# The last graph product with the adjacency tiles as stationary operand: feature rows come out on the partitions, and the bias, the positive part and the layer norm move with it

## What is computed

```python
def _layernorm(x, axis=-1, eps=1e-05):
    m = jnp.mean(x, axis=axis, keepdims=True)
    v = jnp.var(x, axis=axis, keepdims=True)
    return (x - m) / jnp.sqrt(v + eps)
...
x = _layernorm(x + _L0_gnn_ref(x, adj, adj, ...))     # two gated cells, fed by A @ x and by a graph attention
# _L1_gnn_ref(x, adj, adj, ...)
    sim = jnp.tanh(adj * simlar)                      # simlar is adj again
    filt = sim * (adj > 0).astype(sim.dtype)
    ...                                               # the 350 largest of a row: here every row has fewer
    h2 = jnp.tanh(h @ W_proj + b_proj)
    feat = jax.nn.relu(new_adj @ (h2 @ W_gcn) + b_gcn)
x = _layernorm(x + _L1_gnn_ref(x, adj, adj, ...))
```

## Time and profile before

| what | value |
|---|---|
| median of three runs | 1340.59 us |
| the profiled execution, its own time | 1340.1 us |
| its span | 1338.8 us |
| TensorE busy | 1319.6 us, 99% |
| VectorE, ScalarE, GpSimd busy | 1017.7, 961.3, 93.3 us |
| graph products L1363, busy | 167.0 + 27.8 us (448 instructions of 512 columns), 14.1 + 15.8 us (128 of 256) |
| turns of features L1374 | 32 instructions, 5.1 us busy, 4.6 us idle before |
| granted TensorE clock, mean | 0.997 |

### The profile page before, as it was taken

The page is one execution under the profiler, slowest core; times in us unless marked ns, Lnnn a source line. Parts: engine busy times, 40 slices in busy tenths (PEclk is TensorE's granted clock), DMA queues, the critical chain, the costliest instruction groups (busy, mean ns, idle before and its releaser), DMA issues.

```text
span 1338.8 us, 11264 instructions
## 1 busy us (share of the span) xinstructions
PE 1319.6 (99%) x3700; PEld 610.9 (46%) x3700; DVE 1017.7 (76%) x1331; ACT 961.3 (72%) x1087; POOL 93.3 (7%) x188
## 2 busy tenths in 40 slices
PE   8999999999999999999999999999999999999996
PEld 3444444464444444444444444444444454444455
DVE  2533333448798998999989999899968987788883
ACT  4655556238788988889888898898946666565662
POOL 0000001000000100100100100100103441000000
PEclk9999999999999999999999999999999999999998
DMA  9988887353123242332423424223123347888860
GB/s 370 361 288 283 299 290 279 73 206 135 70 95 141 95 160 92 110 141 95 142 94 106 162 79 151 101 94 104 53 94 108 128 146 251 306 292 308 299 219 18
DMA packets 46706, 228.92 MB, mean 171 GB/s; under 512 B 10610, under 2 KB 16434, under 8 KB 21042
## 3 DMA queue, kind: packets, MB, share of 16 engines
q1 hardware_dynamic: 44080, 225.55, 48.0%
q10 hardware_dynamic: 2562, 2.59, 0.6%
HBM read 223.83 MB, written 4.29 MB: 170 GB/s over the span
## 4 chain that ended last, share of the span: by engine, by line
PE 91%; DVE 4%; DMA 2%; POOL 1%; issue 1%; ACT 1%; SPq 0%; DVEq 0%; ACTq 0%; POOLq 0%
PE t_y_ps L1801 48%; PE ns_ps L422 15%; PE t_y_ps L1363 12%; PE t_y_ps L1779 4%; PE rows_ps L1363 3%; PE t_y_ps L1314 2%; DVE mask L1232 2%; PE t_es_ps L1770 2%; DMA pieces<-in_adj_c 2%; PE t_y_ps L1316 1%; PE pos_ps L436 1%; PE rows_ps L1316 1%; PE t_es_ps L1347 0%; DVE mask L1718 0%; PE t_y_ps L1340 0%
## 5 line engine op out<-in xcount | busy, mean ns | idle before, releaser
L1801 PE MATMUL t_y_ps<-mask,x_sb 128*128 128x512 f32 x1536 | 663.1, 592 | 0.3 <-DVE mask L1718 0.3
L1801 PEld LDWEIGHTS t_y_ps<-mask,x_sb 128*128 128x128 f32 x1536 | 290.1, 190 | 364.2 <-issue 343.0
L1718 DVE TENSOR_TENSOR mask<-mask 128x1536 f32<-128x1536 f32 x256 | 451.1, 1763 | 2.0 <-ACT mask L1602 2.0
L1602 ACT ACTIVATE mask<-mask,ones 128x1536 f32<-128x1536 f32 x256 | 400.3, 1564 | 0.0
L1595 ACT ACTIVATE mask<-mask,pieces 128x512 f32<-128x512 f32 x352 | 241.8, 713 | 31.3 <-PE t_y_ps L1801 28.2
L422 PE MATMUL ns_ps<-pieces,x_sb 128*128 128x512 f32 x504 | 226.3, 602 | 6.0 <-DMA pieces<-in_adj_c 5.6
L1704 DVE TENSOR_SCALAR mask<-mask,e_cols 128x512 f32<-128x512 f32 x416 | 189.2, 489 | 56.4 <-PE t_y_ps L1801 45.3
L1363 PE MATMUL t_y_ps<-mask 128*128 128x512 f32 (+1 forms) x448 | 181.2, 562 | 0.1
L422 PEld LDWEIGHTS ns_ps<-pieces,x_sb 128*128 128x128 f32 x504 | 93.8, 192 | 122.1 <-issue 115.6
L288 DVE TENSOR_SCALAR mask<-pieces 128x2048 fp8e4<-128x2048 f32 x64 | 76.9, 1224 | 92.8 <-DMA pieces<-in_adj_c 74.9
L1232 DVE SCALAR_TENSOR_TENSOR mask<-mask 128x2048 f32<-128x2048 f32 x64 | 142.4, 2285 | 0.9 <-DMA mask<-in_adj_c 0.9
(11 more groups left out here) (176 smaller groups left out, 635.3 us busy)
## 6 DMA issues: line engine op xcount, KB each, us to landing
mask<-in_adj_c SPq DMA_DIRECT2D x128, 1024.0 KB, 4.8
pieces<-in_adj_c SPq DMA_DIRECT2D x63, 1024.0 KB, 5.1
mask<-scratch_shifts SPq DMA_DIRECT2D x8, 1536.0 KB, 7.8
x_sb<-in_x_p SPq DMA_DIRECT2D x8, 256.0 KB, 8.9
mask<-in_x_t SPq DMA_DIRECT2D x1, 2048.0 KB, 17.0
pieces<-in_x_t SPq DMA_DIRECT2D x8, 256.0 KB, 2.9
pieces<-scratch_ns_t SPq DMA_DIRECT2D x8, 256.0 KB, 3.7
scratch_ns_t<-ns_sb ACTq DMA_DIRECT2D x7, 256.0 KB, 5.8
```

Of the source, the lines that this page charges most:

```text
L1602: nc.scalar.activation(t, t, ACT.Exp, bias=ones[:, :], scale=-1.0).then_inc(exped, 1)
L1718: nc.vector.tensor_tensor(term(n), term(n), a, ALU.mult).then_inc(terms, 1)
L1801: mm = nc.tensor.matmul(y_ps[c % 2][h][:, :], x_sb[:, k, :], term(n)[:, h, :], start=k == 0, stop=k == NB - 1)
```

## The change

The graph product changes operands. The stationary side is now a 128 x 128 tile of the adjacency block, the moving side g_all[:, k, :], 128 columns; every block takes four products instead of one, and a result tile has its rows on the partitions. Before the first block of a part, one product of contraction length 1 (a row of ones by b_gcn, repeated for each tile) puts the bias in the bank. relu, turn_features and the squarings on ScalarE are gone; add_x1 reads PSUM, takes the positive part and adds x1 in one instruction. Both layer norms are made from bn_stats and bn_aggr per tile (measure), and subtraction and multiplication are one instruction per tile (normalize). The last chunk is cut in three tiles and one, where it was two and two. SyncE loads b_gcn as a row; its waits for the finished parts count tiles.

```diff
-END_PARTS = [... for c in range(NCHUNK - 1)] + [(NCHUNK - 1, q, q + CHUNK // 2) for q in range(0, CHUNK, CHUNK // 2)]
+END_PARTS = [... for c in range(NCHUNK - 1)] + [(NCHUNK - 1, 0, CHUNK - 1), (NCHUNK - 1, CHUNK - 1, CHUNK)]
...
-        def center(i, y, mu, sem_centered):
-            nc.vector.tensor_reduce(mu, y, AX_X, ALU.add)
-            nc.vector.tensor_scalar(mu, mu, 1.0 / H, None, ALU.mult)
-            nc.vector.tensor_tensor(y, y, mu.unsqueeze(2).broadcast_to([P, count, H]), ALU.subtract)
+        def measure(tiles, buf, out, sem_stats, sem_averaged):
+            for t in range(tiles.start, tiles.stop):
+                nc.vector.bn_stats(buf[:, t, :], x1[:, t, :]).then_inc(sem_stats, 1)
+            for t in range(tiles.start, tiles.stop):
+                dve.wait_ge(sem_stats, t + 1)
+                nc.vector.bn_aggr(out[:, t, :], buf[:, t, :]).then_inc(sem_averaged, 1)
+        def normalize(tiles, out, roots, sem_out):
+            for t in range(tiles.start, tiles.stop):
+                nc.vector.tensor_scalar(x1[:, t, :], x1[:, t, :], out[:, t, 0:1], roots[:, t:t + 1], ALU.subtract, ALU.mult)
...
         def add_x1(i):
-            dve.wait_ge(turned2, i + 1)
-            nc.vector.tensor_tensor(x1[:, tiles, :], back_ps[i % 2][...], x1[:, tiles, :], ALU.add)
+            dve.wait_ge(products, NPIECE * (i + 1))
+            nc.vector.scalar_tensor_tensor(x1[:, tiles, :], f_ps[i % len(f_ps)][...], 0.0, x1[:, tiles, :], ALU.max, ALU.add)
...
             if g == 0 and i >= len(f_ps):
-                pe.wait_ge(relu_done, i - len(f_ps) + 1)
+                pe.wait_ge(y2_done, i - len(f_ps) + 1)
+            if g == 0 and tiles.start == 0:
+                pe.wait_ge(bias_step, 9)
+                nc.tensor.matmul(f_ps[i % len(f_ps)][:, q * P:end * P], one_row[:, :],
+                                 b_gcn_row.unsqueeze(1).broadcast_to([1, end - q, H]), start=True, stop=False)
             for j in tiles:
                 k = g * PIECE + j
-                mm = nc.tensor.matmul(f_ps[i % len(f_ps)][:, q * P:end * P], g_all[:, k, :], piece(u)[:, j * CW + q * P:j * CW + end * P],
-                                      start=k == 0, stop=k == NB - 1)
+                for r in range(q, end):
+                    mm = nc.tensor.matmul(f_ps[i % len(f_ps)][:, r * P:(r + 1) * P], piece(u)[:, j * CW + r * P:j * CW + (r + 1) * P],
+                                          g_all[:, k, :], start=False, stop=k == NB - 1 and r == end - 1)
```

More of the change, by code:

```diff
@@ L1025, in make_biases @@
             nc.vector.tensor_copy(gate_bias[k]["hid_n"], b_hid[:, 2:3]).then_inc(bias_step, 1)
+        nc.vector.memset(one_row[:, :], 1.0).then_inc(bias_step, 1)
     def pool_tail(pool):
         for c in range(NCHUNK):
[L1031 to L1034, removed]
+            at, spread, (t, v, out) = POOL_STEPS * c, moments[:, rows(c), 1], (a[:, rows(c)] for a in (newton, var, root))
+            pool.wait_ge(averaged, CHUNK * (c + 1))
+            nc.gpsimd.tensor_scalar(t, spread, 1.0, EPS, ALU.mult, ALU.add).then_inc(rooted, 1)
+            nc.gpsimd.tensor_scalar(v, spread, -0.5, -0.5 * EPS, ALU.mult, ALU.add).then_inc(rooted, 1)
             pool.wait_ge(rooted, at + 2)
@@ L1112, in tanh @@
             nc.scalar.activation(piece(u), piece(u), ACT.Tanh).then_inc(filtered, 1)
[L1114 to L1125, removed]
         act.wait_ge(bias_step, 8)
@@ L1154, in scalar_tail @@
         copy_g(end - 2)
-        square_x(end)
         make_h2(end - 1)
@@ L1215, in make_y @@
             dve.wait_ge(y_done, CHUNK * (c + 1))
-        def center(i, y, mu, sem_centered):
[L1218 to L1223, removed]
+        def measure(tiles, buf, out, sem_stats, sem_averaged):
[6 more added lines that the diff above has]
+            for t in range(tiles.start, tiles.stop):
+                nc.vector.tensor_scalar(x1[:, t, :], x1[:, t, :], out[:, t, 0:1], roots[:, t:t + 1], ALU.subtract, ALU.mult).then_inc(sem_out, 1)
         def finish_x(c):
             dve.wait_ge(rooted, POOL_STEPS * (c + 1))
-            nc.vector.tensor_tensor(x1[:, rows(c), :], x1[:, rows(c), :], root[:, rows(c)].unsqueeze(2).broadcast_to([P, CHUNK, H]),
-                                    ALU.mult).then_inc(x_done, 1)
+            normalize(rows(c), moments, root, x_done)
         def square_a(u):
@@ L1263, in finish_y @@
                 dve.wait_ge(end_root, 2 * (i - ROOT_ON_ACT) + 2)
-            nc.vector.tensor_tensor(x1[:, tiles, :], x1[:, tiles, :], root2[:, tiles].unsqueeze(2).broadcast_to([P, tiles.stop - tiles.start, H]),
-                                    ALU.mult).then_inc(finished, 1)
+            normalize(tiles, moments2, root2, finished)
         for c in range(NCHUNK):
@@ L1272, in vector_tail @@
                 make_y(c - 1)
-                center(c - 1, x1[:, rows(c - 1), :], mean[:, rows(c - 1)], centered)
+                measure(rows(c - 1), stats, moments, stats_made, averaged)
             make_cell("edge", c)
@@ L1283, in vector_tail @@
         make_y(end)
-        center(end, x1[:, rows(end), :], mean[:, rows(end)], centered)
+        measure(rows(end), stats, moments, stats_made, averaged)
         square_a(4)
```

85 lines of the change are left out of this document (27 added, 58 removed).

## The result

The changed kernel takes 1346.62 us (median of five runs, 1345.66 to 1348.06), the kernel before beside it 1341.01 us (1340.47 to 1341.47). The ratio is 1.0042 with an interval of 1.0028 to 1.0057: 5.6 us slower, 0.4%, and twice the forecast 2.8. The profiled execution took 1346.99 us, its span is 1345.7 us.

What follows compares the result with a forecast made beforehand. TensorE, busy 99% of the span, was taken as the bound. Chunks 0 to 6 +10.4 us, last chunk -4.9 and the chain behind it -2.7 gave +2.8 us, forecast 1343.3 us, range 1338.3 to 1350.

Steps and rivals of the forecast that it cites:

- TensorE decides, and more work on it cannot hide: Whole kernel: TensorE is busy 99% of the span; another engine matters only where TensorE waits for it.
- The rate of the pair: New graph product: 2048 pairs of weight load and matmul at 0.1112 us each, +7.0 us over chunks 0 to 6.
- The bias product: Graph stage: two new 512-column instructions per chunk, 0.86 us, +6.0 us over chunks 0 to 6, bounds 0 and that.
- the rate of a train goes by columns: Reason for charging the one-partition product that brings b_gcn the full price per column, 2 x 0.4292 us per chunk.
- The last chunk and the chain behind it: End of graph stage: last chunk 34.4 to 29.5 us (-4.9); after the last matmul 4.53 to 1.8 us (-2.7).
- The stall and the fallen clock: Last chunk before: TensorE stood 4.03 us at chunk 6's turn, then ran slow; both were to go.
- The gate stage: VectorE's new norm takes 2.5 us per chunk against 2.4; net 0, bounds -1.1 and, per chunk without slack, +1.7.
- rival (c): Gate stage: VectorE becomes the bound at 0.34 us for each of twelve instructions per chunk, about 5 us, 1348; chance 0.11.
- (a): New graph product: columns set the pace at 0.109 us a pair, 4.5 us off, 1338.9 or 1337.3 us; chance 0.13.
- (b): Graph stage: the long train cannot be fed with instructions, +20 to +34 us (1363 to 1377); chance 0.09.
- (d): Graph stage: the product bringing b_gcn is cheap because of its one partition, -6 us, 1337.3; chance 0.05.
- my likeliest case: Whole kernel: the forecast holds with small errors, 1340 to 1346.5 us; chance 0.62.

## Why the forecast was right in kind and half too small

- **TensorE decides, and more work on it cannot hide.** Right: no instruction of TensorE in the graph stage waits for anybody, and the whole loss is its own.
- **The rate of the pair.** I took 0.1112 us from the distance to the neighbour's start in the features trains; it is 0.1117. The weight loads in the same group had said 0.112, and I had named them as what sets the beat, yet summed with the other number. 2048 x 0.0005 = 1.0 us. That such a pair stands 2.4 ns above its columns, whichever operand is loaded, is shown by the kernels with 128 and 256 columns; that the load is the cause stays argued, and the distance of the seven loads, which I took for the proof, could not tell it. The Trainium skill (TensorE: Matmul & The Clock Gate, LDWEIGHTS) gives a load its column count over 1.2 GHz, 107 ns for 128; the loads here last 192 ns and are 111.7 ns apart.
- **The bias product.** This term failed. I gave it 0.86 us at most, with zero as its other end; it costs 1.25 at each border of a whole chunk and 1.56 in the last one, together 3.4 us more than forecast and, with 8.8 us for the seven whole chunks, above my upper bound of 6.0. The step that was wrong is "the rate of a train goes by columns": true of the bias product with full tiles, which costs 0.87, not where a tile of one partition stands between full ones.
- **The last chunk and the chain behind it.** -4.1 and -2.7 for -4.9 and -2.7. The stall and the fallen clock went, as forecast; what is missing in the first is the two terms above, 0.7 of bias and 0.1 of rate. bn_stats was priced at 0.29 and is 0.28, bn_aggr at 0.17 and is 0.18 when it stands alone; normalize is 0.35 where I had 0.26. What I did not ask is which edit brings this gain: the experiments put it down to the cut, the place of a turn and the norms, not to the operands.
- **The gate stage.** Forecast 0, measured -1.24 in the changed kernel and -1.3 in the one with the norms alone. The step that was off is VectorE's work for the norm: priced at 2.5 us, it takes 2.10, where work and wait took 2.38 before. Groups of the changed kernel by form (busy, mean ns), then VectorE in chunk 3:

```profile
L1197 DVE TENSOR_SCALAR x_sb<-x_sb,h_moments,h_root 128x128 f32<-128x128 f32 x64 | 17.9, 342 | 4.5 <-POOL h_root L1047 4.2
...
L1190 DVE BATCH_NORM_STATS2 h_stats<-x_sb 128x6 f32<-128x128 f32 x64 | 14.1, 281 | 0.6
...
L1193 DVE BATCH_NORM_AGGREGATE h_moments<-h_stats 128x2 f32<-128x6 f32 x64 | 5.9, 154 | 0.0
...
1036.22 1.11 DVE L1197 TENSOR_SCALAR x_sb<-x_sb,h_moments,h_root 128x128 f32<-128x128 f32 x4
1037.25 1.12 DVE L1183 SCALAR_TENSOR_TENSOR x_sb<-t_y_ps,diag,x_sb 128x128 f32<-128x128 f32 x4
1038.40 0.87 DVE L1190 BATCH_NORM_STATS2 h_stats<-x_sb 128x6 f32<-128x128 f32 x4
1039.19 0.36 DVE L1193 BATCH_NORM_AGGREGATE h_moments<-h_stats 128x2 f32<-128x6 f32 x4
1039.47 0.66 DVE L1166 TENSOR_TENSOR pieces<-pieces 128x512 f32<-128x512 f32 x1
```

By the distances of starts, normalize takes 1.03 us (before, the multiplication 0.61 behind a wait for GpSimd of 0.24), bn_stats and bn_aggr 1.07 (before, center 1.53). The saving adds up over the chunks: from the addition of cells at 1010.75 before (1011.82 after) to the one that the turn of chunk 3 waits for, VectorE takes 37.50 us before and 36.31 after, 1.19 less. The wait for GpSimd is gone up to there (4.2 us in two places remain at the end of the stage, where no one waits behind them), and TensorE's turn of cells in chunk 3, which waited 1.09 us, stands 1.06 behind the start of its neighbour instead of 2.11:

```profile
1047.82 1.02 PE L1313 MATMUL t_y_ps<-mask,pieces 128*128 128x512 f32 x2
...
1048.88 0.66 PE L1298 MATMUL t_y_ps<-ident,pieces 128*128 128x128 f32 x4
```

The 1.24 lies just past the lower bound of my range for this term, 1.1, and rival (c) lay on the wrong side of zero.

- **The rivals.** (a) falls: the columns don't set the pace. (b) falls: trains of 768 pairs keep the beat, and the 12 further instruction transfers leave no gap. (c) falls, (d) has the wrong sign (its -6 also left out the last chunk's bias). The 25 ns per matmul of the Trainium skill (TensorE: Matmul & The Clock Gate, Back-to-back issue gap) are not there either: the pairs lie 2.4 ns above their columns.

Errors of both signs met: +1.0 and +3.4 on TensorE, -1.2 in the gate stage; that they partly cancel is luck. The result lies just above the band of my likeliest case, 1340 to 1346.5. The range held it because rival (c), which did not occur, had pushed its upper end to 1350, not because the main terms' own spread was rightly drawn.

## What to carry to other kernels

Cutting the moving side was nearly free here down to 256 columns (2.5 ns for each further pair) and cost 2.4 ns more per pair at 128; where between the two that begins, no run shows. Keep all stationary tiles of a train at the same number of partitions: filling up the tile of one partition with equal parts took away the whole further cost of 0.38 us per border (zeros instead of equal parts were not tried). Before a gain at the end of a kernel is put down to a new formulation, try the cut, the place of the work and the other edits without it: here they gave all of it.

## What the runs showed of the hardware

- Float32 pairs of weight load and matmul with 128 moving columns stand 0.1117 us apart in trains of 32 to 768 pairs, whichever operand is loaded; with 256 and 512 columns 0.2159 and 0.4292 us. The turns, with shorter loads, stand 0.109 apart.
- A weight load of 1 or of 64 partitions between full tiles is not done beside the matmul ahead of it, nor is the next full one beside its matmuls: some 0.38 us per border, 0 with 128 partitions (64 partitions by one execution).
- bn_stats over 128 columns takes 281 ns on average, four in a row 0.87 us; bn_aggr 154 ns, four in a row 0.36 us. Sum, mean, subtraction and four squarings with a sum over two engines did the same before, in 1.53 us on VectorE and 1.7 us on ScalarE (1039.67 to 1041.39).
